# Spreading one layer norm of the first batch over more attention chunks, and moving two transposes behind it

## The reference

```
x1 = layernorm(x  + o_proj(self_attention(q, k, v of x)))   # 32 heads of 16, 8 key groups, sign weights
x2 = layernorm(x1 + cross_attention(x1, ctx, ctx, mask))    # 512 context keys, no projection
y  = layernorm(x2 + x2 @ W.T + bias)                        # W: 512 x 512, looked up from 4-bit codes
layernorm(x) = (x - mean(x)) / sqrt(var(x) + 1e-5)
```

## Time and profile before

| what | value |
|---|---|
| median of 3 runs | 319.08 us (317.7 to 319.59) |
| the profiled execution | 319.51 us, of which the span in the trace is 317.7 us |
| busy | PE 280.1 us (88%), DVE 238.7 us (75%), ACT 180.1 us (57%), POOL 178.4 us (56%) |
| chain that ended last | PE 60%, DVE 22%, ACT 7%, issue 5% |
| mean granted TensorE clock | 0.945 |

### The profile page before, as it was taken

One profiled execution on the slowest core, in us unless ns is written; L12 is line 12 of the kernel. 1 busy time (PEld: TensorE's weight loads), 2 busy tenths in 40 slices (PEclk: granted clock), 3 DMA queues, 4 the chain that ended last, 5 costly groups with the idle time before them and its releaser, 6 DMA issues.

```text
span 317.7 us, 6204 instructions
## 1 busy us (share of the span) xinstructions
PE 280.1 (88%) x2160; PEld 173.8 (55%) x2160; DVE 238.7 (75%) x644; ACT 180.1 (57%) x316; POOL 178.4 (56%) x276
## 2 busy tenths in 40 slices
PE   7989789877998877699997999999979999998980
PEld 7679344433443442256655665666647676565830
DVE  2768578999758796986569977889899965760836
ACT  2216158859653689456446798777746664366000
POOL 8000188766875097886254988999858863320000
PEclk9999958979797997979999999999997999999997
DMA  7929940678940008400000019200000000000001
GB/s 233 368 91 121 135 45 14 89 99 187 127 86 2 0 16 131 54 3 1 2 1 2 0 43 131 30 3 0 3 0 2 0 3 0 33 35 3 0 0 67
DMA packets 15457, 17.16 MB, mean 54 GB/s; under 512 B 2112, under 2 KB 11456, under 8 KB 15424
## 3 DMA queue, kind: packets, MB, share of 16 engines
q1 hardware_dynamic: 14464, 16.29, 28.2%
q10 hardware_dynamic: 960, 0.46, 0.5%
HBM read 7.05 MB, written 1.05 MB: 25 GB/s over the span
## 4 chain that ended last, share of the span: by engine, by line
PE 60%; DVE 22%; ACT 7%; issue 5%; DMA 3%; SPq 0%; DVEq 0%; POOL 0%; ACTq 0%
PE PT L1142 16%; PE PO L1158 12%; PE PA L1097 7%; DVE mx L902 4%; DMA SM<-in_wq_T 3%; PE PS L1196 3%; PE PA L1100 3%; PE PT L1130 3%; PE PT L1056 3%; ACT PTs L644 3%; DVE SM L898 2%; PE PS L1200 2%; PE PS L1222 2%; PE PS L1234 2%; ACT QA L656 2%
## 5 line engine op out<-in xcount | busy, mean ns | idle before, releaser
L644 ACT ACTIVATE PTs<-PT 128x512 f32<-128x512 f32 x192 | 110.6, 596 | 49.0 <-PE PT L1142 35.4
L586 POOL TENSOR_SCALAR SM<-SM,mx 128x512 f32<-128x512 f32 x128 | 96.5, 765 | 43.9 <-DVE mx L898 42.6
L898 DVE CUSTOM_DVE_ANT_0 SM<-PA,maskq 128x512 f32<-128x512 f32 x128 | 84.8, 686 | 19.0 <-PE PA L1097 18.7
L1142 PE MATMUL PT<-ident,SM 128*128 128x128 f32 x512 | 79.4, 280 | 2.1 <-ACT PTs L644 1.7
L1142 PEld LDWEIGHTS PT<-ident,SM 128*128 128x128 f32 x512 | 60.6, 142 | 25.6 <-issue 10.8
L1097 PE MATMUL PA<-KA,QA 96*128 96x512 bf16 x128 | 49.7, 393 | 6.9 <-DVE mx L898 6.8
L1158 PE MATMUL PO<-PTs,V 128*32 128x256 f32 x768 | 53.2, 395 | 2.4 <-ACT QA L656 2.2
L902 DVE TENSOR_REDUCE mx<-PA 128x2 f32<-128x512 f32 x64 | 41.1, 682 | 14.6 <-PE PA L1100 14.0
L1158 PEld LDWEIGHTS PO<-PTs,V 128*32 128x32 f32 x768 | 20.6, 111 | 24.6 <-issue 8.8
L522 POOL CAST SM<-mx 128x8 bf16<-128x8 f32 x16 | 5.5, 345 | 50.7 <-DVE mx L902 50.7
L1100 PE MATMUL PA<-KA,QA 96*128 96x256 bf16 x128 | 27.1, 307 | 6.9 <-DVE mx L902 5.8
(11 more groups left out here) (166 smaller groups left out, 381.4 us busy)
## 6 DMA issues: line engine op xcount, KB each, us to landing
QA<-parts SPq DMA_DIRECT2D x12, 192.0 KB, 6.7
QA<-x SPq DMA_DIRECT2D x12, 128.0 KB, 4.4
KA<-SM SPq DMA_DIRECT2D x6, 256.0 KB, 12.6
xT<-in_x_T SPq DMA_DIRECT2D x1, 1024.0 KB, 7.4
SM<-in_wq_T SPq DMA_DIRECT2D x1, 1024.0 KB, 10.5
SM<-in_wo_T SPq DMA_DIRECT2D x1, 1024.0 KB, 14.4
x<-in_x_tok SPq DMA_DIRECT2D x1, 1024.0 KB, 7.5
out<-O SPq DMA_DIRECT2D x4, 256.0 KB, 2.1
```

Of the source, the lines that this page charges most:

```text
L586: nc.gpsimd.tensor_scalar(row, row, -1.0, mx[:, u % MX_RING, n:n + 1], ALU.mult, ALU.add).then_inc(sub_done, 1)
L644: nc.scalar.activation(PTs[:, c % PT_RING, j * 512:(j + 1) * 512], PT[:, (2 * c + j) % T_RING, :], ACT.Exp, scale=-1.0 if layer(u) else 1. ...
L898: vec.tensor_tensor_reduce(SM[:, u % SM_RING, n, :], PA[:, f % A_RING, :], maskq[:, n % QT, :], 1.0, LOWEST, ALU.add, ALU.max, mx[:, u % M ...
L1142: last = nc.tensor.transpose(PT[:, n % T_RING, (i % 4) * P:(i % 4 + 1) * P], SM[:, u % SM_RING, i, k * P:(k + 1) * P], ident[:])
```

## The change

```diff
+FEWER_STEPS = {3 * G + 1: 1, 3 * G + 2: 0, 3 * G + 3: 1, 3 * G + 4: 1}
+X2_TURNS = (9, 13)
...
             side_at(at, "norm_x2", t)
-            side_at(at + (5 + 2 * n) * late, "turn_x2", t)
+            side_at(at + X2_TURNS[n] * late, "turn_x2", t)
...
-                    for n in range(max(STEPS[layer(u)], PACE[first_chunk(u) + k])):
+                    steps = FEWER_STEPS.get(u, STEPS[layer(u)])
+                    for n in range(max(steps, PACE[first_chunk(u) + k])):
                         if n < PACE[first_chunk(u) + k]:
                             next(work, None)
-                        if n < STEPS[layer(u)]:
+                        if n < steps:
                             tick()
```

## The result

The changed kernel takes 316.77 us (median of 18 runs, 315.21 to 318.27), the kernel before 319.47 (median of 18). These medians are 2.7 us apart, but single executions of either kernel differ by up to 3 us; the comparison of the two gives a ratio of 0.9942 with a 95% interval of 0.9923 to 0.9962. Of 319.47 that is 1.85 us faster, 1.2 to 2.5, and I use this number. The forecast was 0.9 us faster. Now and then an execution is far slower (one of the 18 of the kernel before took 1450.44 us), and such executions are left out of every ratio here.

What follows compares the result with a forecast made beforehand. DVE, not PE, was taken to bound the edited stretch. 2.2 us earlier, less 0.44 postponed and 0.85 of waiting, gave 0.9 us gained: 318.2 us as a median from 319.08, main range 317.2 to 318.9, overall 316.2 to 320.4.

Steps and rivals of the forecast that it cites:

- (2): Chunks 72 to 80: DVE stays the bound until it catches up; PE's second score of chunk 80 comes 2.2 us earlier.
- The bound: Cross attention around the norm: DVE, not PE, sets the pace; PE lost 4.5 us there, 2.27 of it visible idle time.
- (1): Ahead of chunk 71's first fill, DVE does 8 norm steps instead of 14; PE's 2.27 us idle time goes.
- the term with the wide bounds: DVE time of the norm's 26 steps when spread: 6.75 us, between 5.4 and 8.1.
- the one that I said stays: DVE's work other than the norm, up to the first fill of chunk 79: 19.5 us, unchanged.
- The new waits of PE: Chunks 72 to 80: some 2.7 us of waits in pieces of 0.2 to 1 us; sign to look for 2 to 3.5.
- DVE keeps up: Rival, chance 0.20: merges lose their waits, norm at 5.4 us, DVE no bound in units 26 and 27; gain 2.3 to 3.4.
- the norm's excess: Norm steps' DVE time of 8.1 us above the 5.4 lower bound, put about equally to order and interference with POOL.
- meetings: DVE and POOL colliding on shared SBUF ports; more frequent where the steps go, making the gain 0.6 us smaller.
- (3): Tile 1's later turn: 0.44 us only postponed, plus a PE wait of about 0.85 on the PS bank in chunk 81.
- The clock: Rival, chance 0.17: waits at chunks 80 and 81 totalling about 1.6 us slow the clock, losing 1.5; about 320.3 us.
- No effect: Rival, chance 0.15: norm steps cost the same anywhere and the turn's wait eats DVE's gained idle time; 319.4 us.

Runs made afterwards that it cites:

- the two filled runs: Kernel before with 19, then 9, throwaway matmuls on PE in its idle time in chunk 72; ratios 1.0008 and 0.9987 to the kernel before.
- the packed kernel: Kernel before with 6 norm steps a chunk instead of 3 in chunks 68 to 71; ratio 1.0082 to the kernel before.
- the run with no steps at ends: Changed kernel without norm steps at the ends of chunks in units 25 to 28; ratio 0.9944 to the kernel before.

## Why the prediction was right

The time lies in the stated range and the mechanism is the forecast one, but the gain is twice the forecast's 0.9 us: the sum is off by one term, named under (2), and one of the prediction's own signs missed.

**The bound.** Right. DVE set the pace of this stretch before, and after the change it has no idle time from chunk 68 to 80.

**(1) The long stall goes.** Right. The second score of chunk 72 came 8.33 us after the first fill instead of 11.02, without an idle time.

**(2) Where it goes to.** The method held, one term was off. The forecast had 19.5 us for everything but the norm, 6.75 for the norm's steps, and 26.25 to the first fill of chunk 79; measured are 25.33. The norm, worked out as before: 246.02 - 225.33 = 20.7, less 18 fills at 0.61, four merges at 0.60 to 0.63 and two normalises at 0.31 and 0.32, is 6.6. So the term with the wide bounds was right, and the one that I said stays was wrong by 0.8: it is 18.7. Where rows can be compared, the six merges took 4.2 us from start to start instead of 4.6, the three normalises 1.07 instead of 1.20, and the first fills of chunks 76 and 77 held DVE for 0.61 instead of 0.66. Why the merges are shorter no run shows. I had taken "no instruction changes" for "no duration changes". PE's second score of chunk 80 was thus 3.1 us earlier, not 2.2.

The new waits of PE were forecast at 2.7 us in sum, with 2 to 3.5 as the sign to look for; the trace lists 0.87 in one piece, and 1.35 is what PE lost, by the run with short POOL instructions. The sign missed. The prediction had called itself wrong in the main below 1 us, at a time of 316; the listed wait is below, the loss is not, and with the main part of 0.9 us and the rival "DVE keeps up" at 2.3 to 3.4 the measured 1.85 lies between the two. What PE had lost before was 4.1 us (29.21 - 24.72 - 0.44), not 4.5: its own length of a unit was taken from the last of the three (7.86), but from the turn of unit 24's output (226.24) to that of unit 25's (234.33) it took 8.09 here without any wait for DVE. This didn't enter the sum.

**The split of the norm's excess.** Of the 2.7 us between the bounds, the change took away 1.5 (8.1 to 6.6). Short POOL instructions took away the other 1.2 (6.6 to 5.4), and 0.3 more in the merge of chunk 78. That the 1.5 were the steps' waits for each other is argued, from the long steps beside POOL, which are as many before as after. The rule that the prediction took from the Trainium skill (page "SBUF — State Buffer", section "Who interferes with whom") was right in kind: DVE's steps lose their excess when POOL's instructions are short. That meetings would get more frequent with POOL's busy share, by 0.6 us, no run shows: the long ones in the changed kernel (0.99, 0.52, 0.92) are about as many and as long as before (0.99, 0.63, 0.46).

**(3) The turns.** Right: 0.44 postponed, and a wait of 0.78 idle, 0.94 from when PE would have gone on (254.12 - 252.74 - 0.44), against 0.85. The sum of what was measured, 3.14 - 0.44 - 0.94 = 1.76, is the 1.7 of the stretch and the 1.85 of the medians.

**The rivals.** DVE keeping up didn't happen, since DVE was never idle, but half of its condition did: the merges got 0.4 us shorter, about half of what the forecast was short by. The other half, the norm at its lower bound, did not come. The clock didn't fall behind chunk 81, though 0.87 and 0.78 stood within 5 us and are as long together as the 1.6 us at which the prediction let it fall. "No effect" is excluded by the interval, and the run with the turns alone shows that the steps are the cause. The clock of before as a loss of its own was argued away in the prediction by DVE's backlog; the two filled runs bear this out up to 0.4 us.

## What to carry to other kernels

When one engine runs behind a short ring, look at how much other work stands between two of its ring steps: three fills' worth stopped the other side here, and the same work laid singly between them cost less in itself (6.6 us instead of 8.1), most likely because dependent small steps no longer wait for each other. Side work of the waiting engine belongs where it will wait anyway: a turn moved into such a place was free, the same turn two chunks later, ahead of another user of its only bank, cost 1.4 us. Leave a margin for the producer: PE was in the middle of chunk 80 when DVE finished chunk 78, and a place that was right by count was 0.98 us too early.

## What the hardware showed that I had not expected

In these runs a slow clock cost little where another engine was the bound. The granted clock was 0.50 for 3 us in the kernel before, and filling the idle time kept it at 1.00 and won 0.4 us; in the packed kernel it was 0.50 for over 6 us, outlasted the backlog, and DVE waited 0.58 and 0.93 us for PE. A one-column step of DVE (L947), 0.21 us by itself, took 0.52 in the changed kernel and up to 0.72, in the run with no steps at ends, where POOL worked on full rows, and the final step 0.92 to 0.99 instead of 0.54; with POOL's rows cut to 64 columns all of these were back at 0.21 to 0.22 and 0.54.
